# The two ends of attention in a two-layer transformer kernel: where the last loads, the inversions and the first spread stand

## The reference, cut to what matters

```python
x = x + tanh(g_xattn[0]) * _L0_xattn_ref(_layernorm(x), ctx_1024, ctx_1024, mask, wq, bq, ...)
x = x + tanh(g_ffn[0])   * _L0_ffn_ref(_layernorm(x), ...)      # top-2 of 8 experts
x = x + tanh(g_xattn[1]) * _L1_xattn_ref(_layernorm(x), ctx_1024, ...)
x = x + tanh(g_ffn[1])   * _L1_ffn_ref(_layernorm(x), L1_ffn_weight, L1_ffn_bias)
# in each attention:
weights = softmax(scores); out = einsum('brqk,brkd->brqd', weights, vh); merged @ output_map
```

## Time and profile before

| | |
|---|---|
| Median of 3 runs | 1591.46 us (1590.18 to 1594.08) |
| The profiled execution | 1592.47 us, of which the span of the profile is 1590.7 us |
| TensorE, VectorE, ScalarE, GpSimd busy | 92%, 78%, 64%, 42% |
| Mean granted TensorE clock | 0.953 of full speed |
| Block of attention(0) ends, route begins | 441.05, 441.39 us |
| Block of attention(1) ends, merge begins | 1504.78, 1505.11 us |

### The profile page before, as it was taken

The page is one execution under the profiler, slowest core; times in us unless marked ns, Lnnn a source line. Parts: engine busy times, 40 slices in busy tenths (PEclk is TensorE's granted clock), DMA queues, the critical chain, the costliest instruction groups (busy, mean ns, idle before and its releaser), DMA issues. The chain is left out here.

```text
span 1590.7 us, 29625 instructions
## 1 busy us (share of the span) xinstructions
PE 1462.8 (92%) x11054; PEld 957.8 (60%) x11054; DVE 1242.2 (78%) x1873; ACT 1020.7 (64%) x1761; POOL 662.2 (42%) x1081
## 2 busy tenths in 40 slices
PE   7989999999998599999999999869979999999976
PEld 6863333333387499999999999735523333333455
DVE  6889999999665766666665564369979999999696
ACT  5648999998934444444444444335549998989736
POOL 4315666666222333443442432254415555555030
PEclk9989999999996699999999999979979999999998
DMA  9974444444273222222222221158844444444103
GB/s 287 333 222 103 129 129 129 129 128 129 67 276 108 63 65 85 80 77 90 77 83 87 77 80 38 43 184 283 251 112 125 128 129 128 129 127 129 49 0 107
DMA packets 118749, 198.65 MB, mean 125 GB/s; under 512 B 29568, under 2 KB 63680, under 8 KB 117584
## 3 DMA queue, kind: packets, MB, share of 16 engines
q1 hardware_dynamic: 83840, 111.22, 22.4%
q0 software_dynamic: 33360, 83.94, 18.4%
q10 hardware_dynamic: 1408, 1.61, 0.3%
HBM read 117.77 MB, written 77.87 MB: 123 GB/s over the span
## 5 line engine op out<-in xcount | busy, mean ns | idle before, releaser
L1156 ACT ACTIVATE i_room<-a_ring 128x512 f32<-128x512 f32 x1024 | 547.4, 608 | 57.7 <-PE a_ring L1092 11.3
L351 DVE TENSOR_REDUCE logit<-a_ring 128x2 f32<-128x1024 f32 x416 | 499.7, 1223 | 18.4 <-PE a_ring L345 15.4
L1103 PE MATMUL a_pout<-i_room,values 128*17 128x256 f32 x4096 | 309.1, 386 | 3.3 <-ACT i_room L1156 1.8
L1862 ACT ACTIVATE e_full<-e_pH,b1T 128x320 f32<-128x320 f32 x256 | 135.1, 528 | 245.4 <-PE e_pH L1803 234.7
L1811 PE MATMUL e_pY<-fc_w,e_hid_hi 128*128 128x512 f32 x640 | 237.1, 407 | 0.6 <-DVE e_hid_lo L1917 0.6
L1092 PE MATMUL a_ring<-i_qk 64*128 64x512 f32 x768 | 189.8, 491 | 1.5 <-DVE logit L351 1.4
L1646 POOL DMA_INDIRECT w<-normed,slot_get x80 | 84.0, 1050 | 231.8 <-PE fc_turned L1788 195.6
L1812 PE MATMUL e_pY<-fc_w,e_hid_lo 128*128 128x256 f32 x640 | 179.8, 281 | 0.0
L1103 PEld LDWEIGHTS a_pout<-i_room,values 128*17 128x17 f32 x4096 | 74.6, 95 | 170.5 <-ACT i_room L1156 137.3
L1092 PEld LDWEIGHTS a_ring<-i_qk 64*128 64x128 f32 x768 | 72.5, 186 | 154.5 <-DVE logit L351 110.0
L345 PE MATMUL a_ring<-i_qk 64*128 64x512 f32 x712 | 149.1, 415 | 17.2 <-ACT i_room L1156 12.5
(11 more groups left out here) (360 smaller groups left out, 2510.1 us busy)
## 6 DMA issues: line engine op xcount, KB each, us to landing
ks<-i_room SPq DMA_DIRECT2D x64, 256.0 KB, 4.0
outs<-a_osb SPq DMA_DIRECT2D x64, 256.0 KB, 3.0
qs<-i_room SPq DMA_DIRECT2D x60, 256.0 KB, 4.4
fc_raw<-in_L_ffn_fc_w SPq DMA_DIRECT2D x15, 1024.0 KB, 5.3
i_qk<-ks POOLq DMA_DIRECT2D x84, 128.0 KB, 3.1
i_qk<-qs POOLq DMA_DIRECT2D x84, 128.0 KB, 3.2
BIG<-outs SPq DMA_DIRECT2D x64, 128.0 KB
ytok<-r_zeros SPq DMA_DIRECT2D x8, 1024.0 KB, 9.8
```

The costliest lines, as they stand in the source:

```text
L351: return e.tensor_reduce(nmax[:, :].rearrange("p (x y t) -> p x y t", x=2, y=2)[:, :, p, t], pair[:, :, :], AX.X, ALU.max, negate=True)
L1103: mm = e.matmul(pout[32 * h:32 * h + VW, at], v[:, b * TPB + t, g * HG + h, :], pexp[t][:, h, at], start=(t == 0 and half == 0), stop=(t = ...
L1156: e.activation(pexp[t][:, 2 * p + hh, :], score_bank(n * U + i, hh), ACT.Exp).then_inc(exped, 1)
L1862: e.activation(full[s % 2][:, h * WIDE:(h + 1) * WIDE], pH[h][:, 0:WIDE], ACT.Silu, bias=S.b1T[:, n * KF + f:n * KF + f + 1]).then_inc(act, 1)
```

## The change

It has five parts. (1) The last two pairs of loads, groups 30 and 31, leave the end of attention and are the first thing SP issues in route and in merge; the semaphores of the stores (`sent`) and the tiles `osb` now outlive the stage for that. (2) The LATE reciprocal is VectorE's first instruction in route and merge, ahead of the first update. (3) The spread of batch 0 stands ahead of the last two value units of attention, in other banks of `ring`. (4) In attention(1) the EARLY reciprocal and its two cuts stand inside `quantise_weight`, ahead of the wait for GpSimd. (5) One semaphore, `divided`, replaces `inverted` and `low`.

```diff
@@ class Division
+        self.osb = [sb(f"osb{j}", [P, SEQ]) for j in range(2)]
+        self.sent, self.sent_before = S.sent, l * 16 * B * G // 2
+    def load_outputs(self, e, n):
+        back = self.back[EARLY if n // G < EARLY_BATCHES else LATE]
+        e.wait_ge(self.sent[n % 2], self.sent_before + 16 * (n // 2 + 1))
+        e.dma_start(out_rows(self.S, n // G, n % G), self.outs[n, :, 0:DH, :]).then_inc(back, 16)
+        e.dma_start(self.den[n * HG:(n + 1) * HG, :], self.outs[n, :, DH, :]).then_inc(back, 16)
+    def load_last_outputs(self, e):
+        load_last = B * G - 2, B * G - 1
+        for n in load_last:
+            self.load_outputs(e, n)
@@ attention
         def spread_bank(b, kd):
-            return ring[:, b * KD + kd, :]
+            return ring[:, (2 * (PAIRED + NG * U - 1) + 2 + b * KD + kd) % BANKS, :]
@@ attention, sync
                 store_outputs(NG - 1)
-                load_outputs(NG - 2)
-                load_outputs(NG - 1)
@@ attention, tensor
                 for i in range(U - VALUE_LAG, U):
+                    if i == U - 2:
+                        for kd in range(KD):
+                            division.spread_rows(e, spread_bank(0, kd), 0, kd)
                     values(NG - 1, i // 2, i % 2)
-                for b in range(SCALED_AHEAD):
+                for b in range(1, SCALED_AHEAD):
@@ attention, vector
                     e.tensor_reduce(wmax[:, :], w[:, :, :], AX.XY, ALU.max, apply_absolute_value=True).then_inc(c.up(), 1)
+                    invert_early()
                     e.wait_ge(wred, 1)
@@ attention, vector
                 if l == 1:
                     quantise_weight()
-                division.invert(e, EARLY)
-                division.copy_high(e, EARLY)
-                division.cut_low(e, EARLY)
+                else:
+                    invert_early()
@@ route, sync
+                division.load_last_outputs(e)
                 e.wait_ge(zeroed, 1)
@@ route, vector
+                division.invert(e, LATE)
                 for i in range(B):
@@ route, vector
                     nb.stats(e, i, i % 2, x)
-                    if i == 0:
-                        division.invert(e, LATE)
@@ merge
+            @block.sync
+            def _(e):
+                division.load_last_outputs(e)
@@ merge, vector
+                division.invert(e, LATE)
                 for b in range(B + 1):
                     if b < B:
                         update(b)
-                        if b == 0:
-                            division.invert(e, LATE)
```

More of the change, by code:

```diff
@@ L112, in build @@
         S.stage_sems, S.sems_ctx = [], ExitStack()
+        S.sent = [S.sem(f"sent{j}") for j in range(2)]
         def sb(name, shape, dt=F32):
@@ L901, in __init__ @@
         self.pick = sb("pick", [P, P, DH], F32R)
+        self.osb = [sb(f"osb{j}", [P, SEQ]) for j in range(2)]
+        self.sent, self.sent_before = S.sent, l * 16 * B * G // 2
+        self.outs = S.outs[l]
         self.back = [S.sem(f"d{l}_back{j}") for j in range(2)]
-        self.inverted, self.high, self.low, self.picked, self.spread, self.scaled = (
-            S.sem(f"d{l}_{x}") for x in ("inverted", "high", "low", "picked", "spread", "scaled"))
+        self.divided, self.high, self.picked, self.spread, self.scaled = (
+            S.sem(f"d{l}_{x}") for x in ("divided", "high", "picked", "spread", "scaled"))
+    def load_outputs(self, e, n):
[7 more added lines that the diff above has]
+            self.load_outputs(e, n)
     def make_pick(self, e):
@@ L912, in invert @@
         e.wait_ge(self.back[part], 2 * 16 * G * batches)
-        e.reciprocal(self.rec[self.ROWS[part], :], self.den[self.ROWS[part], :]).then_inc(self.inverted, 1)
+        e.reciprocal(self.rec[self.ROWS[part], :], self.den[self.ROWS[part], :]).then_inc(self.divided, 1)
     def cut_high(self, e, part):
-        e.wait_ge(self.inverted, part + 1)
+        e.wait_ge(self.divided, 2 * part + 1)
         e.activation(self.parts[HI][self.ROWS[part], :], self.rec[self.ROWS[part], :], ACT.Copy).then_inc(self.high, 1)
     def copy_high(self, e, part):
-        e.wait_ge(self.inverted, part + 1)
+        e.wait_ge(self.divided, 2 * part + 1)
         e.tensor_copy(self.parts[HI][self.ROWS[part], :], self.rec[self.ROWS[part], :]).then_inc(self.high, 1)
@@ L925, in cut_low @@
         e.wait_ge(self.high, part + 1)
-        e.tensor_tensor(self.parts[LO][rows, :], self.rec[rows, :], self.parts[HI][rows, :], ALU.subtract).then_inc(self.low, 1)
+        e.tensor_tensor(self.parts[LO][rows, :], self.rec[rows, :], self.parts[HI][rows, :], ALU.subtract).then_inc(self.divided, 1)
     def scale(self, e, src, b, k):
@@ L935, in spread_rows @@
             e.wait_ge(self.picked, 1)
-            e.wait_ge(self.low, 1)
+            e.wait_ge(self.divided, 2)
         if b == EARLY_BATCHES and k == 0:
-            e.wait_ge(self.low, 2)
+            e.wait_ge(self.divided, 4)
         rows = self.ROWS[EARLY] if b < EARLY_BATCHES else slice(0, P)
@@ L960, in attention @@
         nmax, nparts, nT = inputs.nmax, inputs.nparts, inputs.nT
-        osb = [sb(f"osb{j}", [P, SEQ]) for j in range(2)]
         ring = ps("ring", [P, BANKS, SEQ])
@@ L976, in attention @@
         scored, exped, summed, taken = (sem(x) for x in ("scored", "exped", "summed", "taken"))
-        oput = [sem(f"oput{j}") for j in range(2)]
+        osb, oput = division.osb, division.sent
         def max_first(m):
@@ L1013, in store_outputs @@
                     e.dma_start(S.outs[l][n, :, :, :], osb[n % 2][:, :]).then_inc(oput[n % 2], 16)
[L1015 to L1019, removed]
                 def load_first(n):
@@ L1035, in _ @@
                     if n >= 2:
-                        load_outputs(n - 2)
+                        division.load_outputs(e, n - 2)
                 store_outputs(NG - 1)
-                load_outputs(NG - 2)
-                load_outputs(NG - 1)
             @block.gpsimd
@@ L1144, in take_outputs @@
                     if n >= 2:
-                        e.wait_ge(oput[n % 2], 16 * (n // 2))
+                        e.wait_ge(oput[n % 2], division.sent_before + 16 * (n // 2))
                     e.activation(osb[n % 2][:, :], pout[:, :], ACT.Copy).then_inc(taken, 1)
@@ L1178, in turn_maxima, with invert_early @@
                     e.transpose(nT[n % 2][:, :], nparts[n % 2][:, :].bitcast(F32)).then_inc(nturned, 1)
+                def invert_early():
+                    division.invert(e, EARLY)
+                    division.copy_high(e, EARLY)
+                    division.cut_low(e, EARLY)
                 def quantise_weight():
```

## The result

The changed kernel takes 1596.95 us (median of 7 runs, 1596.07 to 1600.54), the kernel before 1591.46 us (7 runs). The ratio is 1.0036, 95% interval 1.0027 to 1.0046: slower by 5.5 us, where 1592.4 and a range to 1595.2 were forecast. The profiled execution took 1600.54 us (span 1598.8 us), the highest of the seven, so its lengths are compared by stage, not by its end.

A forecast was written before the change was run, and what follows sets the result against it. VectorE's scales were taken to bound attention's ends, TensorE route and VectorE merge. Route -0.1 and merge +1.05 gave +0.95 us on 1591.46, so 1592.4 us; the 8-in-10 range was 1589.2 to 1595.2.

The forecast's parts named there:

- the landing: Route and merge: the last loads land at S + 5.4 (S = stage start), bounds S + 4.75 and S + 5.7.
- Merge: In merge: a later start of VectorE's busy chain plus a wait, 1.05 us lost; bounds 0.4 and 1.35.
- the low part: In merge: VectorE waits 0.5 us ahead of it, having 4.36 us of work in a 4.84 us gap.
- 0.55 us lost: In merge: VectorE's busy chain starts at 1509.4 instead of 1508.84, 0.55 us lost.
- GpSimd's lateness: In merge: GpSimd's first instruction came 2.5 us after its input; with the input later, this is hidden.
- Route: In route: the first update comes later, but TensorE turns its rows 0.1 us sooner; -0.1 us.
- In route the reciprocal hides it: In route: TensorE's stretch at clock 0.81 may fall elsewhere, hidden by the reciprocal; counted in 1 us of scatter.
- TensorE idle in route behind the third output product: In route: a sign in the new profile that would show the prediction wrong; no size given.
- The blocks end 1.0 us earlier each: At the end of both attentions: blocks end 1.12 us earlier, the last values moving 0.1 us later.
- The early reciprocal and its cuts: In attention(1): they take 4.7 us and fit in VectorE's 5.41 us wait for GpSimd.
- the queue shared with zeros: In route: last loads share with 1 MB stores; 2.5 us more, 1594.9, chance 0.1; with two, 1597.5, chance 0.05.
- Quick loads: In route and merge: the loads land at S + 3.9; gain 1.6 us, 1589.9, chance 0.2.

The follow-up runs named there:

- Without B: The change with the late reciprocal back behind the first statistics in route and merge: 1590.10 us, ratio 0.9988 to the kernel before.
- without A: The change with the last two pairs of loads issued at the end of attention, as before: 1592.23 us, ratio 1.0003 to the kernel before.
- a third pair: The change with another, unused pair of loads issued ahead of the two and awaited by the reciprocal: 1601.38 us, ratio 1.0055 to the kernel before.
- the sums first: The change with the small loads of sums issued first and the late reciprocal waiting for them alone: 1589.18 us, ratio 0.9972 to the kernel before.

## Why the prediction was wrong

**The cause** is shown from four sides. Without B the loss goes, without A it goes, a third pair enlarges it, and with the sums first it goes while all moves stay. It is the reciprocal's wait for the loads of the same stage, whose length the two of 128 KB set. The last experiment changed both their place in the queue and the semaphore, so it doesn't say which of the two was needed.

**The step that failed** is the landing: "I take S + 5.4, nearer to the second, which is the same pair of transfers". VectorE was released at S + 6.3 to S + 6.7, outside both bounds (S + 4.75 and S + 5.7). I read landing off the transfer view, as the last byte moved; this came at S + 5.7 to S + 5.95, as the worse bound had it or a little over, but VectorE started 0.6 to 0.9 us later. The bound had no term for that.

The Trainium skill, page "DMA: Bandwidth & Descriptors", section "Anatomy of one DMA", says of transfers that GpSimd issues that most of the fixed cost of about 2.0 us goes by between the last byte and the semaphore. I had used that page's total, for transfers that SP issues, and not this part of it. The trace agrees in kind, with 0.6 to 0.9 us here; for the whole landing the measurement decides: S + 6.3 to S + 6.7, where the estimate from that page's total was S + 3.9.

**Merge** was right in mechanism. The first update starts at S + 9.97 (1519.52) where it started 3.73 us after the stage's start. Less the 3.35 us that the reciprocal no longer takes behind it, and with 0.71 us ahead of the low part (0.5 forecast), that makes 3.6 us; the stage is 3.5 us longer. The term was "0.55 us lost" plus 0.5, net of the block's end; with the landing measured it is 3.5 - 1.0 = 2.5 us. GpSimd's lateness was hidden, as forecast: its first instruction, at 1522.77, starts 0.1 us behind its input.

**Route** was priced at -0.1 us, net of the block's earlier end. Here a second step failed: "In route the reciprocal hides it", which put TensorE's clock at nothing. That holds for the first two products alone. Up to its last part route is 54.2 us long against 50.8 in the first profile of before: 3.4 us more, 2.4 net. The late landing is 1.1 us of the difference to the forecast. About 1.3 us more come from the clock: the third product (S + 11.3, behind a wait of 3.66 us) starts 2.2 us later in the stage than before, takes 5.38 us at 0.68 instead of 3.62, and the fourth starts 3.4 us later. The prediction's own times had TensorE idle ahead of the third product, by 1.2 us (449.05 to 450.3), and gave the clock behind it no price. The sign that it named, "TensorE idle in route behind the third output product", isn't quite what came: the idle time is ahead of that product.

My baseline was also one execution, and I put its stretch at 0.81 in the scatter. Before, route takes 65.3 us in one profile and 61.6 in the other, 1.65 us of it from the first two products and 2.1 from the last part, each by the clock. After, it took 66.8 and 67.0.

**The sum.** By stages the change costs 1.6 + 3.5 - 2.0 = 3.1 us against the first profile of before, and 5.3 + 1.8 - 2.0 = 5.1 us against the second. Measured were 5.5. In the first comparison the change gets 2.0 us back in route's last part, which ran at 0.69 and not at 0.51; without that part the sum is 3.4 + 3.5 - 2.0 = 4.9 us. Whether the late reciprocal is what raises the clock there isn't shown. How often an execution has the one or the other route isn't known from two profiles, and the two profiled executions of the change themselves lie 5.4 us apart (1600.54 and 1595.17), with 120.6 and 114.8 us until attention's first exponential. So the split of the remaining 2.4 us stays open; nothing else in the profiles of the change is longer in a way that its neighbours without the loss don't show.

**What was right.** The blocks end 1.0 us earlier each (1.12 forecast; the last values moved by 0.2, not 0.1). The early reciprocal and its cuts fit beside GpSimd, with 0.88 us of the wait left. Of the rivals, the queue shared with zeros was named for a loss of this size, but it isn't the cause: merge has no zeros and its reciprocal starts at S + 6.6, in route with them at S + 6.5. Quick loads (S + 3.9) didn't come while the large ones stood ahead; for the sums alone S + 2.1 to S + 2.6 came.

## What to carry to other kernels

An instruction that stands first in a stage and waits for transfers of the same stage pays their full landing, less what its engine would have waited for anyway: count from the issue to the first instruction that the semaphore released, never to the last byte, and add each transfer ahead of it. If it needs only the small one, issue that first and give it a semaphore of its own; here this turned a loss of 0.36% into a gain of 0.28%. And before a stage is priced from one profile, look whether its clock is the same in another.

## What was not expected of the hardware

- Two loads of 8 KB, issued back to back, released their reader 2.1 to 2.6 us after the first issue; the same loads interleaved with two of 128 KB did so after 6.3 to 6.7 us.
- A third pair cost 1.2 to 1.5 us, less than the 2.1 us between the ends of two pairs in attention.
- TensorE's first two products of route ran at a clock of 0.81 in one profile and at 1.00 in another of the same kernel, behind nearly the same wait (1.73 and 1.76 us). Over all 14 profiles they took 7.14 or 7.15 us in 7 of the 8 where that wait was 1.46 or 1.47 us, and 8.7 to 8.8 us in 5 of the 6 where it was 1.73 to 2.26 us. The third product, behind a wait of 3.66 us, ran at 0.68 (0.69 in the change's second profile).
- Route's last part ran at a clock of 0.50 or 0.51 in eight profiles, at 0.69 to 0.71 in five and at 0.60 in one. All four profiles with the reciprocal first in route and two pairs of large loads to wait for, wherever these were issued, are among the five.
- The time until attention's first exponential was 114.8 to 120.6 us over 14 profiles of kernels with the same first stage, so a profile's end says less than its stages.
